# Message stage of a graph network: two rings in place of one, the difference of odd pairs completed in PSUM, DVE left with the even pairs

## The chip, the cores and the metric

The kernel runs on one core of a Trainium2 chip. The metric is the device time of one launch in microseconds (us), lower is better. The engines named here are PE (TensorE, matmuls into PSUM), DVE (VectorE), ACT (ScalarE), POOL (GpSimd) and SP (SyncE, which issues plain DMAs). PSUM is the memory that PE writes; it is read by DVE and ACT.

## The reference, cut to what matters

Two graph layers follow each other on 6250 nodes with 256 features and 100000 edges. The second one is the message layer, and the stage that is changed computes this for every edge (row, col):

```
xy   = clip(mink_dot(x[row], x[col]) + K, None, -EPS) - K
u    = x[col] + xy * x[row] * C
dist = sqrt(sqdist(x[row], x[col]))
x_local_tangent = proj_tan(dist * u / max(mink_norm(u), MIN_NORM), x[row])
h    = silu(concat(x_tangent[row], x_tangent[col], distances) @ att_w1 + att_b1)
att  = sigmoid(h @ att_w2 + att_b2) * edge_mask
agg  = segment_sum(x_local_tangent * att, row, N) / NORM_FACTOR
```

For an edge the kernel needs the node row of the far end (gathered by index), the node row of the near end (edges are sorted by it), their difference, a sum of squares of it, the attention input, and a weighted sum per near node.

## The kernel before

The message stage (`messages`) goes over the sorted edges in steps of 128 edges. Two steps (SPAN = 2) that share a block of near nodes are a **pair**; four pairs (SG = 4, eight steps, G = 8) are a **turn**, and two turns (WG = 2) a **window**. There are 110 turns, so 55 windows and 440 pairs. Every engine has its own program, written as a function `period(t)` for each turn t; engines meet by semaphores, and each works through its own program strictly in that order. Pairs are numbered p = 0 to 3 within a turn; 0 and 2 are called even, 1 and 3 odd.

- POOL gathers, for each step, 128 rows of 514 numbers from `d_xr` into a ring `far` of five turns (RING = 5), by `gather_pair`, L2216 to L2226. A row holds 257 numbers for the difference, one node term, and 256 for attention. A slot of the ring is freed by `out_in`, which PE sets at the very end of the pair's life.
- SP loads the index columns (`col`) and a row of local node numbers per edge (`hotT`); DVE turns `hotT` into a one-hot matrix (`hot_columns`, L2421).
- PE, `near(t, p)` (L2284 to L2306), spreads the near nodes' rows to the edges by one-hot matmuls: `near_a` (257 wide, L2301) and `near_c` (256 wide, L2302). For odd pairs an identity matmul (L2304) adds the gathered attention part onto `near_c` in PSUM. `near_a` has four banks, so two pairs fit; `near(t, p)` waits until what `near` wrote two pairs earlier has been read. An even pair takes four matmuls, an odd pair six. `sums(t, p)` (L2308 to L2322) adds up the finished edges per node, two matmuls (L2321).
- DVE, `differences` (L2403 to L2414): for every pair, gathered row plus `near_a`, in place in the ring (L2410), and for even pairs gathered part plus `near_c` (L2413). Further attention sums (L2443), weights (`hot_rows`, L2433), accumulation (`add`, L2454), and once per window the small chain `angles`, `radii`, `shares`.
- ACT: `silu` for every pair (L2346 from PSUM for odd, L2349 for even pairs), `squares` (L2361), and once per window `chain` (L2364 to L2374) between `silu(t, 1)` and `squares(t, 1)`: five short activations on 16 numbers per partition with three table loads.
- POOL, once per window: `place_a` (two copies), then `finish`, eleven small operations, each waiting for the one before.

In PE's program of a turn t these stand in a row: sums, near(t, 2), sums, near(t, 3), sums, near(t+1, 0), sums, near(t+1, 1). The sums are those of the turn LAG = 3 turns back.

Of the kernel before, what the change touches and what calls it, by code (L numbers as in the profile page):

```python
# [7 lines left out]
F32 = mybir.dt.float32  # L8
# [2103 lines left out]
def messages(nc, m, edges):  # L2112
# [8 lines left out]
    with Stage(nc, "ms") as ctx:  # L2121
# [3 lines left out]
        SLOT = G * XW  # L2125
        IN_AREA = 3
        more = sb("more", [P, (RING - IN_AREA) * SLOT])
        spare = [m.area[:, n * SLOT:(n + 1) * SLOT] for n in range(IN_AREA)] + [more[:, n * SLOT:(n + 1) * SLOT] for n in range(RING - IN_AREA)]
        far = [t.rearrange("p (k c) -> p k c", c=XW) for t in spare]
        rest = [IN_AREA * SLOT]  # L2130

        def rest_of_area(n):
# [3 lines left out]

        WSLOTS = BODY // WG
        r_aw2 = rest_of_area(DIM)
        given = rest_of_area(2 * WSLOTS * WSTEPS).rearrange("p (v w k) -> p v w k", v=2, w=WSLOTS)
# [3 lines left out]
        SQ, AL = (given[:, v] for v in range(2))  # L2143
# [14 lines left out]
        got = [ctx.gather_sem(m, f"got{h}") for h in range(RING)]  # L2158
        (c_in, made, hotT_in, near_in, apart, squared, v_in, silu_in, al_in, dv, ab_in, root_in, nn_in, norm_in, ex_in, z_in, ln_in,
         rden_in, a_in, pl, c_ready, weighted, out_in, summed) = (sem(n) for n in (  # L2160
             "c_in", "made", "hotT_in", "near_in", "apart", "squared", "v_in", "silu_in", "al_in", "dve", "ab_in", "root_in", "nn_in",
# [10 lines left out]
        def pair_before(t, p, back):  # L2172


            q, r = divmod(p - back, SG)
            return t.plus(q), r

        with nc.Block() as block:
            @block.sync
            def _(sp):  # L2180
# [15 lines left out]
                def fetch(t):  # L2196
                    fetch_col(t.plus(2))
# [6 lines left out]
                fetch_col(Turn(0, 0))  # L2204
                fetch_col(Turn(0, 1))
# [3 lines left out]
            def _(pool):  # L2209
# [7 lines left out]
                def gather_pair(t, p):  # L2217
                    if not t.exists():
                        return
                    if p == 0:  # L2220
                        reach(col_in[t.h], (t.i + 1) * 16)
                    if t.plus(-RING).exists():
                        reach(out_in, t.plus(-RING).n * SG + p + 1)
                    for k in (SPAN * p, SPAN * p + 1):
                        pool.indirect_dma_start(out=far[t.slot][:, k, :], out_offset=None, in_=m.d_xr,  # L2225
                                                in_offset=bass.IndirectOffsetOnAxis(ap=col[:, t.h, k, 0:1], axis=0)).then_inc(got[t.slot], 16)  # L2226

                def place_a(w):

                    reach(nn_in, w.window + 1)  # L2230
                    for t in (w, w.plus(1)):
                        k0 = (t.h % WG) * G
                        GP.tensor_copy(far[t.slot][:, :, DIM], A[:, k0:k0 + G]).then_inc(a_in, 1)

                def finish(w):

                    n = w.window
                    sm = PoolSmall(m, pool, GP, Links(pool, pl, n * PER))
                    reach(root_in, 2 * n + 2)
                    sm.ts(FLAG, A, 0.01, None, ALU.is_lt)  # L2240
                    sm.ts(S, A, 3.0 / 160, -1.0 / 12, ALU.mult, ALU.add)
                    sm.tt(S, S, A, ALU.mult)
                    sm.ts(S, S, 1.0, None, ALU.add)
                    sm.tt(S, S, ROOT, ALU.mult)
                    reach(ln_in, n + 1)
                    sm.tt(S, S, LN, ALU.subtract)
                    sm.tt(S, S, FLAG, ALU.mult)
                    sm.tt(S, S, LN, ALU.add)
                    sm.ts(S, S, math.sqrt(FAR), None, ALU.min)
                    reach(rden_in, 2 * n + 2)  # L2250
                    sm.tt(S, S, DEN, ALU.mult)
                    assert sm.ln.n == PER, sm.ln.n
# [5 lines left out]
                def period(t):  # L2258
# [3 lines left out]
                    if w:  # L2262
                        place_a(w)
                    gather_pair(t.plus(2), 1)
                    if w:
                        finish(w)
# [345 lines left out]
```

## Time and profile before

| | us |
|---|---|
| median of 3 runs | 4565.07 |
| lowest, highest | 4560.52, 4568.45 |
| the profiled execution | 4568.81 |
| its span in the trace | 4566.7 |
| message stage, first to last near matmul | 2562.0 to 4285 |

The message stage is a bit over a third of the span; the sorting and the attention stage are ahead of it, a short final stage follows. A fp32 matmul of the program stands in the trace as two records ("x2"). The duration of a PE record has the drain of the array in it, so records overlap; the pace is read from start to start. The granted clock of PE is given as a fraction: 1.00 is 2.4 GHz and 0.50 is 1.2 GHz.

### The profile page before, as it was taken

How to read it: one execution, taken by the hardware profiler on the slowest of the kernel's cores; microseconds unless marked ns; L12 is line 12 of the kernel's file. 1: busy time of each engine (PE TensorE's matmuls, PEld its weight loads, DVE VectorE, ACT ScalarE, POOL GpSimd, SP SyncE). 2: the span in 40 equal slices, each digit the busy share in tenths (PEclk: the TensorE clock that was granted, in tenths of full speed). 3: DMA queues.
4: the chain of work that ended last, by engine and by line, in shares of the span. 5: the costliest groups of instructions: out<-in, count | busy, mean ns of one | idle time of the engine just before them, and what ended most of it. 6: DMA issues, size and time to landing. Idle time of an engine off the chain costs nothing. (4 is left out here: it accounts for less than half of the span.)

```text
span 4566.7 us, 61946 instructions
## 1 busy us (share of the span) xinstructions
PE 3026.1 (66%) x12512; PEld 2401.1 (53%) x12513; DVE 3592.1 (79%) x9543; ACT 2065.8 (45%) x5079; POOL 2032.7 (45%) x2519
## 2 busy tenths in 40 slices
PE   1101111465887877778746688888888888888685
PEld 0101110454665655556635577676766767677554
DVE  6879998554999999999976477777777777777766
ACT  0013332002555555555546455555555555555356
POOL 1000000003777777777710466565656665565301
PEclk9997555787899999999978899999999999999888
DMA  0010000325887888887844566656556565665531
GB/s 7 0 37 0 0 0 16 91 80 160 243 240 243 241 238 240 240 243 238 247 112 132 167 172 173 167 160 172 164 169 171 164 170 161 173 173 161 127 81 45
DMA packets 294449, 664.33 MB, mean 145 GB/s; under 512 B 77025, under 2 KB 146335, under 8 KB 293869
## 3 DMA queue, kind: packets, MB, share of 16 engines
q0 software_dynamic: 141312, 463.96, 35.3%
q1 hardware_dynamic: 152813, 197.34, 15.4%
q14 instruction: 278, 2.28, 0.2%
q8 instruction: 46, 0.75, 0.1%
HBM read 616.23 MB, written 44.91 MB: 145 GB/s over the span
## 5 line engine op out<-in xcount | busy, mean ns | idle before, releaser
L1812 POOL DMA_INDIRECT big<-d_qv,at_col x880 | 930.5, 1057 | 572.7 <-DMA at_col<-by_dst_edge_cols 290.5
L2225 POOL DMA_INDIRECT big<-d_xr,ms_col x528 | 530.3, 1004 | 588.7 <-DMA ms_col<-by_src_edge_cols 259.2
L2301 PE MATMUL ms_near_a<-big,ms_hotT 128*128 x1760 | 575.0, 410 | 232.4 <-DMA big<-d_xr,ms_col 123.1
L2302 PE MATMUL ms_near_c<-big,ms_hotT 128*128 x1760 | 561.3, 402 | 0.0
L1858 PE MATMUL at_out<-at_pv,at_hot 128*128 128x264 f32 x1760 | 518.8, 421 | 4.9 <-DVE big L2024 3.1
L2301 PEld LDWEIGHTS ms_near_a<-big,ms_hotT 128*128 128x128 f32 x1760 | 345.6, 202 | 323.6 <-issue 276.1
L1838 PE MATMUL at_kx<-big 128*128 x1760 | 493.3, 407 | 31.8 <-ACT big L1912 23.2
L2225 POOL DMA_INDIRECT ms_more<-d_xr,ms_col x352 | 353.8, 1005 | 214.7 <-PE ms_out L2321 111.6
L1838 PEld LDWEIGHTS at_kx<-big 128*128 128x128 f32 x1760 | 350.8, 204 | 111.1 <-issue 54.2
L2302 PEld LDWEIGHTS ms_near_c<-big,ms_hotT 128*128 128x128 f32 x1760 | 357.6, 203 | 58.0
L2433 DVE TENSOR_SCALAR ms_hot<-ramp,ms_col,big 128x128 f32<-128x128 f32 x880 | 269.1, 374 | 145.1 <-POOL big L2255 143.4
L1858 PEld LDWEIGHTS at_out<-at_pv,at_hot 128*128 128x128 f32 x1760 | 335.1, 203 | 69.7 <-issue 10.5
L2003 DVE TENSOR_TENSOR big<-big,at_kx 128x512 f32<-128x512 f32 x440 | 297.2, 676 | 73.4 <-DMA big<-d_qv,at_col 41.5
L2321 PE MATMUL ms_out<-big,ms_hot 128*128 128x257 f32 x1056 | 280.6, 389 | 31.4 <-DVE ms_hot L2433 29.5
L2410 DVE TENSOR_TENSOR big<-big,ms_near_a 128x514 f32<-128x514 f32 x264 | 178.4, 676 | 117.5 <-DMA big<-d_xr,ms_col 94.3
L1922 ACT ACTIVATE at_hot<-ramp,at_col 128x128 f32<-128x128 f32 x880 | 267.4, 386 | 3.8 <-PE at_out L1858 3.8
L1982 DVE TENSOR_TENSOR at_pv<-big,at_pw 128x1024 f32<-128x1024 f32 x220 | 268.0, 1218 | 0.0
L2014 DVE TENSOR_REDUCE at_sc<-big 128x32 f32<-128x1024 f32 x220 | 265.4, 1207 | 0.1
L2361 ACT ACTIVATE ms_junk<-big 128x255 bf16<-128x255 f32 x528 | 211.7, 402 | 109.8 <-DVE big L2410 109.1
L2321 PEld LDWEIGHTS ms_out<-big,ms_hot 128*128 128x128 f32 x1056 | 201.7, 194 | 77.2 <-DVE ms_hot L2433 16.5
L532 POOL DMA_INDIRECT by_src_got<-by_src_rec,by_src_tile_i x4 | 3.8, 945 | 524.2 <-DVEq L402 523.3
L2024 DVE SCALAR_TENSOR_TENSOR big<-big,at_keep,at_out 128x264 f32 x440 | 211.6, 481 | 20.1 <-PE at_out L1858 10.2
(368 smaller groups left out, 6693.6 us busy)
## 6 DMA issues: line engine op xcount, KB each, us to landing
big<-by_dst_marks SPq DMA_DIRECT2D x110, 512.0 KB, 5.4
ms_hotT<-by_src_marks SPq DMA_DIRECT2D x110, 448.0 KB
big<-d_qv,at_col POOLq DMA_INDIRECT x880
d_qv<-big SPq DMA_DIRECT2D x5, 2240.0 KB, 9.1
big<-d_xr,ms_col POOLq DMA_INDIRECT x528, 4.2
ms_hotT<-by_src_marks SPq DMA_DIRECT2D x110, 60.0 KB
d_xr<-mid_hm SPq DMA_DIRECT2D x5, 1128.8 KB, 6.9
ms_more<-d_xr,ms_col POOLq DMA_INDIRECT x352, 4.2
```

The lines of the kernel that those rows point to most:

```text
L1812: pool.indirect_dma_start(out=ring[t.slot][:, k, :], out_offset=None, in_=m.d_qv, in_offset=bass.IndirectOffsetOnAxis(ap=col[:, t.h, k, 0: ...
L1838: last = TE.matmul(kx[:, p, k * DIM:(k + 1) * DIM], hotT[:, t.h % 2, (SPAN * p + k) * P:(SPAN * p + k + 1) * P], m.keys[:, bass.ds(at, DIM ...
L1858: last = TE.matmul(out[:, p % 2, 0:AW], hot[:, t.h % 2, j, :], pv[:, t.h % 2, j].rearrange("p h d -> p (h d)"), start=(k == 0), stop=(k == ...
L1922: A.activation(hot[:, t.h % 2, k, :], m.ramp[:, :], ACT.Abs, scale=-1.0, bias=col[:, t.h, k, 1:2].bitcast(F32)).then_inc(far_rows, 1)
L1982: V.tensor_tensor(pv[:, t.h % 2, k, :, 0:DH], ring[t.slot][:, k, DIM:2 * DIM].rearrange("p k (h d) -> p k h d", d=DH), pw[:, t.wslot, k0:k ...
L2003: V.tensor_tensor(prod[:, SPAN * p:SPAN * p + SPAN, :], ring[t.slot][:, SPAN * p:SPAN * p + SPAN, 0:DIM], kx[:, p, :].rearrange("p (a d) - ...
L2014: V.tensor_reduce(sc[:, k0:k0 + G // 2, :].rearrange("p k h -> p (k h)"), prod[:, k, :].rearrange("p k (h d) -> p (k h) d", d=DH), axis=AX ...
L2225: pool.indirect_dma_start(out=far[t.slot][:, k, :], out_offset=None, in_=m.d_xr, in_offset=bass.IndirectOffsetOnAxis(ap=col[:, t.h, k, 0:1 ...
L2301: TE.matmul(near_a[:, (SPAN * p + k) % 4, 0:TW], rows, m.tab_a[:, bass.ds(at, TW)], start=True, stop=True)
L2302: last = TE.matmul(near_c[:, p % 2, k * DIM:(k + 1) * DIM], rows, m.tab_c[:, bass.ds(at, DIM)], start=True, stop=p % 2 == 0)
L2321: last = TE.matmul(out[:, p % 2, 0:TW], hot[:, j, :], far[t.slot][:, j, 0:TW], start=(k == 0), stop=(k == SPAN - 1))
L2433: V.tensor_scalar(hot[:, k, :], m.ramp[:, :], col[:, t.h, k, 1:2].bitcast(F32), cs[:, t.wslot, at:at + 1], ALU.is_equal, ALU.mult).then_in ...
```

## The change

The one ring of five turns is split in two. The gathered rows go into a ring of ten pairs (`far_rows`), and each slot is freed when the pair's attention sums are done (`al_in`). The differences go into a second ring of five turns with rows of 257 (`dd`). Since the node term does not get a place in `dd`, ACT copies it out of the gathered row (`keep_node_term`) once per pair, and `place_a` becomes two copies in ACT's `chain`. For odd pairs PE adds the gathered 257 numbers onto `near_a` by the identity, and ACT copies the whole difference from PSUM into `dd`; DVE does `differences` for even pairs only. POOL's window chain is laced with six gathers, and its order is different. Gathers are issued by two more pairs ahead, waits for gathered rows are per pair, and `sums` and `hot_rows` run LATE = 4 turns back where they ran 3.

```diff
+        PAIRS, DSLOT, LATE = 10, G * TW, WG + 2
+                    if k == 0:
+                        before, q = pair_before(t, p, PAIRS)
+                        if before.exists():
+                            reach(al_in, before.n * G + SPAN * q + SPAN)
...
                     before, q = pair_before(t, p, 2)
                     if before.exists():
-                        pe.wait_ge(apart, before.n * SG + q + 1)
+                        pe.wait_ge(apart_odd if p % 2 else apart, before.n * (SG // 2) + q // 2 + 1)
...
                         if p % 2:
-                            last = TE.matmul(near_c[...], m.ident[:, :], far[t.slot][:, SPAN * p + k, XB:XW],
+                            TE.matmul(near_a[...], m.ident[:, :], far_rows(t, p)[:, k, 0:TW], start=False, stop=True)
+                            last = TE.matmul(near_c[...], m.ident[:, :], far_rows(t, p)[:, k, XB:XW],
                                              start=False, stop=True)
...
                 def squares(t, p):
-                    act.wait_ge(apart, t.n * SG + p + 1)
+                    if p % 2:
+                        AC.activation(dd[t.slot][:, SPAN * p:SPAN * p + SPAN, :], near_a[:, SPAN:2 * SPAN, 0:TW], ACT.Identity).then_inc(apart_odd, 1)
+                        act.wait_ge(apart_odd, t.n * (SG // 2) + p // 2 + 1)
+                    else:
+                        act.wait_ge(apart, t.n * (SG // 2) + p // 2 + 1)
...
                 def chain(w):
                     AC.activation(NN, NN, ACT.Sqrt).then_inc(norm_in, 1)
+                    for t in (w, w.plus(1)):
+                        AC.copy(dd[t.slot][:, :, DIM], A[:, (t.h % WG) * G:(t.h % WG) * G + G]).then_inc(a_in, 1)
...
                     for p in range(SG):
-                        differences(t, p)
+                        if p % 2 == 0:
+                            differences(t, p)
```

**PE, one odd pair between two `sums`.** Names: `hotT` is the one-hot matrix, `ident` the identity, `near_a` and `near_c` the two PSUM targets, `ms_out` the target of `sums`. The even pairs are unchanged. After the change:

```order
L2354 MATMUL ms_out<-big,ms_hot 128x257 x2
L2333 ISA
L2333 MATMUL ms_near_a<-big,ms_hotT 128x257
L2334 ISA
L2334 MATMUL ms_near_c<-big,ms_hotT 128x256
L2336 MATMUL ms_near_a<-big,ident 128x257
L2337 MATMUL ms_near_c<-big,ident 128x256
L2333 MATMUL ms_near_a<-big,ms_hotT 128x257
L2334 MATMUL ms_near_c<-big,ms_hotT 128x256
L2336 MATMUL ms_near_a<-big,ident 128x257
L2337 MATMUL ms_near_c<-big,ident 128x256
L2354 MATMUL ms_out<-big,ms_hot 128x257 x2
```

The two rows of L2336 are new, the others stood there before.

**ACT, from `silu(t, 1)` through the window's chain to `squares(t, 1)`, before:**

```order
L2346 ACTIVATE big<-ms_near_c 128x2x256
L2366 ISA
L2367 ACT_TABLE_LOAD
L2367 ACTIVATE big<-big 128x16
L2368 ACTIVATE big<-big 128x16
L2370 ACTIVATE big<-big 128x16
L2371 ISA
L2372 ACT_TABLE_LOAD
L2372 ACTIVATE big<-big,ms_nb 128x16
L2374 ACT_TABLE_LOAD
L2374 ACTIVATE big<-big,ones 128x16
```

The same place after the change, from the chain's first activation on:

```order
L2411 ACTIVATE big<-big 128x16
L2412 ACTIVATE big<-big 128x16
L2414 ACTIVATE big<-big 128x16
L2416 COPY ms_more<-big 128x8 x2
L2418 ACT_TABLE_LOAD
L2418 ACTIVATE big<-big,ms_nb 128x16
L2420 ACT_TABLE_LOAD
L2420 ACTIVATE big<-big,ones 128x16
L2396 ACTIVATE ms_more<-ms_near_a 128x514
L2405 ACTIVATE ms_junk,big<-ms_more 128x255 x2
L2376 COPY big<-big 128x2
```

The copies of L2416 came from POOL; the copy of L2396, which empties an odd pair's `near_a`, stands behind the chain, and the node term's copy of L2376 ahead of each silu.

**POOL, the window's chain after the change**, with the gathers (DMA rows of L2240) between its operations:

```order
L2259 TENSOR_SCALAR big<-big 128x16
L2260 TENSOR_SCALAR big<-big 128x16
L2240 DMA big<-d_xr,ms_col 128x514
L2263 TENSOR_TENSOR big<-big 128x16
L2240 DMA big<-d_xr,ms_col 128x514
L2266 TENSOR_SCALAR big<-big 128x16
L2240 DMA big<-d_xr,ms_col 128x514
L2269 TENSOR_TENSOR big<-big 128x16
L2240 DMA big<-d_xr,ms_col 128x514
```

Before, the eleven operations of the chain stood in a row with no gather between them.

## Rows read from the trace of the kernel before

**Rows 1.** The page, part 1: busy us (share of the span) xinstructions.

```profile
PE 3026.1 (66%) x12512; PEld 2401.1 (53%) x12513; DVE 3592.1 (79%) x9543; ACT 2065.8 (45%) x5079; POOL 2032.7 (45%) x2519
```

**Rows 2.** Busy time by stretch (x records), PEclk is the granted clock; 50 windows.

```profile
2708.20:4259.05 1550.85, 1321.73 (x5488) 1094.62 (x5488) 1188.90 (x4313) 855.64 (x2401) 941.38 (x1422) 0.93 0.60 168
```

**Rows 3.** Waits of PE in that stretch: us in total, times, longest.

```profile
PE ms_near_a L2301 <- DMA big<-d_xr,ms_col: 110.1, 30, 4.4
PE ms_near_a L2301 <- DMA ms_more<-d_xr,ms_col: 66.6, 19, 4.5
PE ms_out L2321 <- DVE ms_hot L2433: 35.4, 54, 3.1
```

**Rows 4.** Timeline of PE: start, us, line, records, [idle before <-releaser].

```profile
3309.42 1.03 PE L2321 MATMUL ms_out<-ms_more,ms_hot 128*128 128x257 f32 x4
3313.66 1.17 PE L2301 MATMUL ms_near_a<-big,ms_hotT 128*128 x2 [3.21 <-DMA ms_more<-d_xr,ms_col]
...
3317.61 0.60 PE L2304 MATMUL ms_near_c<-ms_more,ident 128*128 128x256 f32 x2
3318.04 1.03 PE L2321 MATMUL ms_out<-ms_more,ms_hot 128*128 128x257 f32 x4
3318.91 0.59 PE L2301 MATMUL ms_near_a<-big,ms_hotT 128*128 x2
...
3320.64 1.03 PE L2321 MATMUL ms_out<-big,ms_hot 128*128 128x257 f32 x4
3321.51 0.60 PE L2301 MATMUL ms_near_a<-big,ms_hotT 128*128 x2
```

**Rows 5.** Timeline of ACT at the same window, silu(t, 1), chain, squares(t, 1).

```profile
3318.24 0.60 ACT L2346 ACTIVATE ms_more<-ms_near_c 128x512 f32<-128x512 f32 x1 [1.93 <-PE ms_near_c L2304]
3318.86 1.28 ACT L2367 ACT_TABLE_LOAD   x1
...
3320.39 0.20 ACT L2370 ACTIVATE big<-big 128x16 f32<-128x16 f32 x1
3320.60 1.28 ACT L2372 ACT_TABLE_LOAD   x1
...
3323.52 0.31 ACT L2374 ACTIVATE big<-big,ones 128x16 f32<-128x16 f32 x1
3323.73 0.40 ACT L2361 ACTIVATE ms_junk<-ms_more 128x255 bf16<-128x255 f32 x1
```

**Rows 6.** PSUM reads by ACT: a copy in the final stage (ns min/median/max), L2346 by mean.

```profile
L1517 ACT ACTIVATE fin_sl<-fin_p x25: 594/603/604, 4351.0 to 4524.3; 128x512 f32<-128x512 f32 x25
L2346 ACT ACTIVATE big<-ms_near_c 128x512 f32<-128x512 f32 x132 | 77.4, 586 | 61.9 <-PE ms_near_c L2304 60.7
```

**Rows 7.** Stretches as in Rows 2, and PE's timeline ahead of two of them.

```profile
3314.00:3316.00 2.00, 2.00 (x6) 1.56 (x6) 1.97 (x11) 1.11 (x4) 1.70 (x2) 0.50 0.85 261
3990.00:3993.00 3.00, 3.00 (x9) 2.36 (x8) 3.00 (x12) 2.01 (x7) 2.50 (x4) 0.50 0.32 90
3671.00:3674.00 3.00, 3.00 (x16) 2.63 (x15) 3.00 (x12) 1.93 (x4) 1.16 (x2) 1.00 0.17 64
...
3988.18 1.13 PE L2321 MATMUL ms_out<-big,ms_hot 128*128 128x257 f32 x4 [2.52 <-DVE ms_hot L2433]
3670.60 1.13 PE L2321 MATMUL ms_out<-big,ms_hot 128*128 128x257 f32 x4 [2.01 <-DVE ms_hot L2433]
```

**Rows 8.** DVE: groups of instructions (busy us, mean ns, idle before), one wait.

```profile
L2410 DVE TENSOR_TENSOR big<-big,ms_near_a 128x514 f32<-128x514 f32 x264 | 178.4, 676 | 117.5 <-DMA big<-d_xr,ms_col 94.3
DVE ms_hot L2433 <- POOL big L2255: 134.6, 49, 3.9
```

**Rows 9.** POOL: its longest wait, and two rows of its timeline.

```profile
POOL big L2225 <- PE ms_out L2321: 166.6, 78, 6.0
3308.79 0.95 POOL L2225 DMA_INDIRECT ms_more<-d_xr,ms_col  x1 [0.30 <-issue]
3333.76 1.05 POOL L2225 DMA_INDIRECT big<-d_xr,ms_col  x1 [0.59 <-issue]
```

More of the change, by code:

```diff
@@ L2124, in messages @@
         sem = ctx.sem
[L2125 to L2130, printed above, removed]
+        PAIRS, DSLOT, LATE = 10, G * TW, WG + 2
+        far = m.area[:, 0:PAIRS * SPAN * XW].rearrange("p (k c) -> p k c", c=XW)
+        rest = [PAIRS * SPAN * XW]
+        more = sb("more", [P, (RING - 1) * DSLOT])
         def rest_of_area(n):
@@ L2215, in reach, with gather @@
                     pool.sem_inc(m.nothing, 1)
-                def gather_pair(t, p):
+                def gather(t, p, k):
                     if not t.exists():
                         return
[L2220 to L2235, printed above, removed]
-                    n = w.window
-                    sm = PoolSmall(m, pool, GP, Links(pool, pl, n * PER))
-                    reach(root_in, 2 * n + 2)
[L2240 to L2244, printed above, removed]
+                    if k == 0:
+                        if p == 0:
+                            reach(col_in[t.h], (t.i + 1) * 16)
+                        before, q = pair_before(t, p, PAIRS)
+                        if before.exists():
+                            reach(al_in, before.n * G + SPAN * q + SPAN)
@@ new lines, in gather, with gather_pair, finish_and_gather, settle @@
+                    pool.indirect_dma_start(out=far_rows(t, p)[:, k, :], out_offset=None, in_=m.d_xr,
+                                            in_offset=bass.IndirectOffsetOnAxis(ap=col[:, t.h, SPAN * p + k, 0:1], axis=0)).then_inc(got[far_slot(t, p)], 16)
+                def gather_pair(t, p):
+                    gather(t, p, 0)
+                    gather(t, p, 1)
+                def finish_and_gather(w, t):
+                    n = w.window
+                    two, three = t.plus(2), t.plus(3)
+                    ln = Links(pool, pl, n * PER)
+                    def settle():
+                        ln.wait()
+                        pool.sem_inc(m.nothing, 1)
+                    reach(root_in, 2 * n + 2)
+                    reach(nn_in, n + 1)
+                    ln.mark(GP.tensor_scalar(FLAG, A, 0.01, None, ALU.is_lt))
+                    ln.mark(GP.tensor_scalar(S, A, 3.0 / 160, -1.0 / 12, ALU.mult, ALU.add))
+                    gather(two, 2, 0)
+                    settle()
+                    ln.mark(GP.tensor_tensor(S, S, A, ALU.mult))
+                    gather(two, 2, 1)
+                    settle()
+                    ln.mark(GP.tensor_scalar(S, S, 1.0, None, ALU.add))
+                    gather(two, 3, 0)
+                    settle()
+                    ln.mark(GP.tensor_tensor(S, S, ROOT, ALU.mult))
+                    gather(two, 3, 1)
+                    settle()
@@ L2270, in _ @@
+                for n in range(2 * SG + 1):
                     gather_pair(Turn(0, n // SG), n % SG)
@@ L2320, in sums @@
                         j = SPAN * p + k
-                        last = TE.matmul(out[:, p % 2, 0:TW], hot[:, j, :], far[t.slot][:, j, 0:TW], start=(k == 0), stop=(k == SPAN - 1))
+                        last = TE.matmul(out[:, p % 2, 0:TW], hot[:, j, :], dd[t.slot][:, j, 0:TW], start=(k == 0), stop=(k == SPAN - 1))
                     last.then_inc(out_in, 1)
                 def period(t):
-                    old = t.plus(-LAG)
+                    old = t.plus(-LATE)
                     for p in range(SG):
@@ L2360, in squares @@
                         at = (t.h % WG) * G + SPAN * p + k
-                        AC.activation(junk[:, k, 1:DIM], far[t.slot][:, SPAN * p + k, 1:DIM], ACT.Square,
+                        AC.activation(junk[:, k, 1:DIM], dd[t.slot][:, SPAN * p + k, 1:DIM], ACT.Square,
                                       accum_out=SQ[:, t.wslot, at:at + 1]).then_inc(squared, 1)
```

101 lines of the change are left out of this document (59 added, 42 removed).

## The prediction

> **What bounds the kernel now.** I read the busy shares first, and they mislead: DVE has the most work over the whole span and PE comes second [rows 1], but that is a mean over stages. So I went to the stage that is changed, and there to a regular stretch of 50 windows. It lasts 1550.85 us, 31.0 us per window; in it PE is busy 1321.7 us, DVE 1188.9, POOL 941.4 and ACT 855.6 [rows 2]. PE is the bound, at 85%. What the reader should look for next is what fills the other 15%. Of PE's waits [rows 3] the gathered rows make up 110.1 + 66.6 = 176.7 us in 49 waits, one per window and 3.6 us each; the wait of `sums` for DVE's weights makes 35.4 us. With about 0.3 us of small ones that is 4.6 us per window.
>
> The work itself: from start to start, the four records of `sums` take 3318.91 - 3318.04 = 0.87 us and the eight of an even pair 1.73 us [rows 4], which is 0.2165 us per record or 0.433 us per matmul. A window has four even pairs (4 matmuls), four odd ones (6) and eight sums (2), 56 matmuls, so 24.2 us. Then 31.0 = 24.2 + 4.6 + 2.2. The rest of 2.2 us is the drain ahead of each wait (about 0.17 us, three waits) and the clock. After the wait of 3.21 us PE ran at 0.50, the level of 1.2 GHz [rows 7], and the odd pair that takes 6 x 0.433 = 2.6 us took 3318.04 - 3313.66 = 4.38 us [rows 4]: 1.8 us lost per window.
>
> **What the change takes away.** (1) The gathered rows come too late now because POOL waits for `sums` to free a slot, 166.6 us into one of its two buffers alone [rows 9]. After the change a slot is freed by the attention sums, and ten pairs make 10/8 of a window, about 40 us, while a pair needs two gathers (start to start 0.95 + 0.30 = 1.25 us each [rows 9]), a few us to land and some 8 us until its attention sums. I put this wait at nothing, -3.6 us per window. (2) The weights are needed one turn later (15 us), and they were late by 134.6/49 = 2.7 us on DVE [rows 8]. That wait goes too, about -0.8 us per window on PE with the small ones. (3) DVE loses four operations of 0.68 us per window [rows 8], which on an engine at 77% of the stage is worth nothing by itself.
>
> **What it adds on PE.** Two identity matmuls of 257 columns per odd pair, eight per window: 8 x 0.433 = 3.5 us. Nothing hides them, since they stand in PE's own row. PE's floor is then 64 x 0.433 = 27.7 us per window. With (1) and (2) and nothing else it would be 27.9, a gain of 3.1 us per window. The decision lies in the next term.
>
> **The wait it adds.** `near(t, 3)` must find the banks of odd pair (t, 1) empty. Until now DVE emptied them and ACT's `silu(t, 1)` the other half, both ahead of the chain. Now the copy that empties `near_a` stands on ACT behind the chain, so once per window PE waits for the chain. Behind the waiting `near(t, 3)` are all of PE's later sums and pairs, and behind these DVE and ACT.
> Take as zero the drained end of `near(t, 1)`, here 3317.61 + 0.60 = 3318.21 [rows 4]. ACT starts silu at 3318.24 [rows 5], +0.03. The new node term copy ahead of it is a short activation; the nearest is one of 16 numbers, 0.20 us by itself, 0.11 when the next overlaps it [rows 5]: I take 0.15. Silu until the first table load 0.62, from there until the chain is done 3323.73 - 3318.86 = 4.87. The two copies that came from POOL: 0.11 to 0.20 each, 0.3 together. The new copy of 128x514 out of PSUM: 0.59 to 0.60 by the two nearest rows [rows 6], and 0.05 to hand over. Sum 6.6 us. PE meanwhile has one sums, one even pair and one sums, which end 3.3 us after the zero (3321.51 - 3318.21 [rows 4]). So `near(t, 3)` starts 3.3 us late. Bounds: copies free and 0.55 us for the large one give 2.9, all of them at twice my value and DVE late for the chain by 0.5 give 4.7.
> Can something else hold ACT less? The chain cannot start earlier, it stands behind `silu(t, 1)`, which waits for the end of `near(t, 1)`. DVE's part comes in time: after the end of `near(t, 0)` it has 1.2 us of differences, 0.7 of attention sums and some 2.5 of `angles`, done 4.4 us later, while ACT ends `silu(t, 1)` 4.3 + 0.8 = 5.1 us after it (PE needs 3.46 + 0.87 for the odd pair and the sums ahead of it). At (t+1, 1) and (t, 3) no chain is in between and the copy comes within 1.5 us, under 3.3 us of PE work: no wait there.
>
> The Trainium skill speaks on this term ("ScalarE: Activation LUTs", section "What ACT_TABLE_LOAD costs"): a switch of tables costs a load of 1283 ns and a drain of about 1380 ns, 2.66 us in all. The load agrees with the row (1.28 us); the drain does not show here, since the load starts 0.02 us after the 0.60 us activation ended and the next load 0.01 us after 0.20 us. By the page's price the chain would take some 4 us more and the wait would be 7 us; I go by the rows.
>
> **The clock.** The added wait shows as about 3.2 us of idle PE. Of PE's waits in this stage of 2.5 us and more, the shortest of them 2.52 us, all but one were followed by a stretch at 0.50, and the shorter ones were not; one of each kind stands at 3988 and 3670, with the stretch behind it [rows 7]. The odd pair at 3313.66 lost 1.8 us. I take 1.7 for a wait that is a little shorter than most of those before; bounds 0 and 2.2.
>
> **The sum.** Per window 27.7 + 3.3 + 1.7 + 0.1 for small waits = 32.8 us, against 31.0: +1.8, or for 55 windows +97 us (with 1.7 it is +93; I take +95). At the start of the stage PE waits for one pair's rows in place of a turn's: four gathers fewer, 4 x 1.25 = -5 us. At the end one more turn of sums is left over, at 0.9 to 1.3 us a pair partly beside the last chain: +2 us. Sum +92. The profiled execution took 4568.8, so it would take 4661; the median is 3.7 us lower, which gives **4657 us**, 2% slower.
>
> ACT's own load is no bound: 855.6/50 = 17.1 us plus four copies of 0.6 and ten short ones of 0.15 makes 21 of 32.8. DMA moves the same bytes in more time.
>
> **The rivals.**
> (a) The wait is there, the clock stays up. Then the window is 31.1 us, +0.1 x 55 - 3 = +3 us: **4568**, no change. It needs a wait under 2.5 us, or 3 us that count as too short. For it: the phase at which PE stops. Against: every wait of 2.5 to 3.2 us save for one was followed by a fall. Chance 0.08.
> (b) PE runs back to back. The window is 27.9 us, 3.1 x 55 = 170 us less, with the start 173: **4392**. It decides at 3.3 us: only if ACT is through from `near(t, 1)` to the large copy within that time, while the chain alone takes 4.87. Partly so, by a shorter chain or an earlier start that I overlook, anything from 4400 to 4550. Chance 0.12 for the two.
> (c) POOL becomes the bound. Its window chain now alternates six gathers with operations: a gather after a small operation comes 0.59 in place of 0.30 us after it [rows 9], so a step is about 0.95 + 0.25 + 0.22 + 0.59 = 2.0 us, six make 12; ten gathers more 12.5, the last operations 2.5: 27 us of 32.8, and each pair waits for the attention sums. If a step costs 3 us (a wait in it, or the operation drained first), POOL needs 33 us and its waits come on top: 34 us per window, +3 x 55 = +165, **4730**. Against: the ring's slack of some 20 us. Chance 0.16, with all else that makes it slower still, as the load of `hotT` coming late for `hot_columns`, which now has 6 to 9 us where it had 12.
> (d) That the change does not do what it says: excluded by the order of the instructions, where L2336 and L2396 stand.
>
> **How the numbers follow.** The forecast has 0.64, with 4620 to 4700 by its bounds (window 32.1 to 33.6). About 9 us (0.2%) is what a measurement of this kernel can tell from no change. Slower by more: 0.64 + 0.16 = 0.80. Same: 0.08. Faster: 0.12. The range must hold 0.8: 0.62 of the forecast, (a) whole, and the larger part of (c), so 4560 to 4735.
>
> **What would show it.** PE's waits: none for gathered rows, one per window of about 3.2 us of `near_a` for ACT's copy of L2396, and its mean at 0.60 us. PE records in the stage go from 112 to 128 per window. The granted clock stays near 0.93, with one fall per window. DVE's wait for POOL is gone, and DVE waits for PE and ACT. If the wait per window is under 2.5 us, or no fall follows, I am wrong towards (a); if PE's longest wait is another one, towards (c).

## The result, and the profile after

The changed kernel took 4676.47 us (median of 4 runs, 4661.82 to 4688.16), the kernel before 4563.21 us (4 runs, 4560.52 to 4568.45). The ratio is 1.0245, with a 95% interval of 1.0213 to 1.0278: 2.4% slower. The forecast was 4657 us in a range of 4560 to 4735. The profiled execution took 4671.57 us (span 4669.7), 103 us more than that of before, where the sum had +92.

The busy times of the page, part 1 (us, share of the span, instructions), to be read against [rows 1]:

```profile
PE 3200.0 (69%) x13392; PEld 2577.2 (55%) x13393; DVE 3488.8 (75%) x9323; ACT 2249.2 (48%) x5849; POOL 2045.1 (44%) x2409
```

DVE has 220 instructions and 103 us less; PE has 880 more records of matmuls and ACT 770 more instructions: 440 short copies, 220 large ones and the 110 that POOL had. These are the groups of part 5 that were added (records, busy us, mean ns, idle time before):

```profile
L2336 PE MATMUL ms_near_a<-big,ident 128*128 128x257 f32 x880 | 291.2, 415 | 0.0
L2376 ACT COPY big<-big 128x2 f32<-128x2 f32 x440 | 84.3, 192 | 675.3 <-PE ms_near_c L2337 341.2
```

The regular stretch, here 53 windows (us, then busy time and records of PE, weight load, DVE, ACT and POOL, granted clock, DMA share, GB/s), answers [rows 2]:

```profile
2623.48:4363.20 1739.72, 1565.93 (x6657) 1331.33 (x6656) 1166.30 (x4372) 1080.89 (x3277) 1005.34 (x1407) 0.93 0.58 159
```

That is 1739.72/53 = 32.8 us per window, where [rows 2] had 31.0. PE is busy 90% of it. What fills the rest is in PE's waits over the whole stage (2560 to 4400; us in total, times, longest):

```profile
PE ms_near_a L2333 <- ACT ms_more L2396: 144.2, 44, 4.8
PE ms_near_a L2333 <- ACT big L2396: 24.1, 10, 3.3
PE ms_near_a L2333 <- DVE ms_hotT L2463: 17.6, 1, 17.6
PE ms_out L2354 <- DVE ms_hot L2475: 17.5, 11, 3.4
PE ms_near_a L2333 <- DMA big<-d_xr,ms_col: 2.5, 2, 1.7
```

[rows 3] has the regular stretch of before; over the whole stage (2560 to 4300) the same waits there were:

```profile
PE ms_near_a L2301 <- DMA big<-d_xr,ms_col: 123.1, 33, 6.6
PE ms_near_a L2301 <- DMA ms_more<-d_xr,ms_col: 73.4, 21, 4.5
PE ms_out L2321 <- DVE ms_hot L2433: 39.3, 57, 3.1
```

The waits for gathered rows, 123.1 + 73.4 = 196.5 us before, are gone but for 2.5 us at the start. In their place PE waits for ACT's large copy, 144.2 + 24.1 = 168.3 us in 54 waits, one per window: 3.1 us each. The weights hold PE for 17.5 us in place of 39.3.

One such wait can be followed through both engines. PE's timeline (start, us, line, tile, records, idle time before and its releaser), from the end of the odd pair (t, 1):

```profile
3123.24 0.60 PE L2337 MATMUL ms_near_c<-big,ident 128*128 128x256 f32 x2
3123.68 1.03 PE L2354 MATMUL ms_out<-ms_more,ms_hot 128*128 128x257 f32 x4
3124.55 0.59 PE L2333 MATMUL ms_near_a<-big,ms_hotT 128*128 x2
...
3126.28 1.03 PE L2354 MATMUL ms_out<-big,ms_hot 128*128 128x257 f32 x4
3130.57 0.70 PE L2333 MATMUL ms_near_a<-big,ms_hotT 128*128 x2 [3.27 <-ACT ms_more L2396]
```

ACT's timeline in the same time:

```profile
3123.88 0.19 ACT L2376 COPY big<-big 128x2 f32<-128x2 f32 x1 [1.49 <-PE ms_near_c L2337]
3123.98 0.59 ACT L2385 ACTIVATE big<-ms_near_c 128x512 f32<-128x512 f32 x1
3124.59 1.28 ACT L2411 ACT_TABLE_LOAD   x1
...
3126.22 0.29 ACT L2416 COPY ms_more<-big 128x8 f32<-128x8 f32 x2
3126.52 1.28 ACT L2418 ACT_TABLE_LOAD   x1
...
3129.44 0.31 ACT L2420 ACTIVATE big<-big,ones 128x16 f32<-128x16 f32 x1
3129.65 0.58 ACT L2396 ACTIVATE ms_more<-ms_near_a 128x514 f32<-128x514 f32 x1
```

`near(t, 1)` ends at 3123.24 + 0.60 = 3123.84, and PE has work until 3126.28 + 1.03 = 3127.31. ACT starts 0.04 us after the pair's end, goes through silu and the chain with no gap, and starts the copy at 3129.65; PE starts 0.92 us after that. PE then goes on within 0.34 us of the copy's end at 3130.23: ACT is what it waits for.

### The profile page after: what moved, and what is told of

It reads as the page before. It is cut to its first block and busy times, and to the rows that moved or that the text cites. A ratio compares the mean times of both kernels' runs of the same rounds, so it can differ in the third digit from the quotient of the medians.

```text
span 4669.7 us, 63970 instructions
## 1 busy us (share of the span) xinstructions
PE 3200.0 (69%) x13392; PEld 2577.2 (55%) x13393; DVE 3488.8 (75%) x9323; ACT 2249.2 (48%) x5849; POOL 2045.1 (44%) x2409
## 5 line engine op out<-in xcount | busy, mean ns | idle before, releaser
L2240 POOL DMA_INDIRECT big<-d_xr,ms_col x880 | 902.6, 1026 | 868.7 <-DVE big L2485 406.2
L2333 PE MATMUL ms_near_a<-big,ms_hotT 128*128 x1760 | 568.9, 406 | 188.5 <-ACT ms_more L2396 144.2
L2496 DVE SCALAR_TENSOR_TENSOR big<-big,ms_keep,ms_out 128x257 f32 x440 | 210.5, 478 | 290.8 <-PE ms_out L2354 278.6
L2485 DVE CUSTOM_DVE_ANT_0 big<-big 128x256 f32<-128x256 f32 x880 | 337.6, 421 | 101.5 <-ACT big L2389 101.0
L2376 ACT COPY big<-big 128x2 f32<-128x2 f32 x440 | 84.3, 192 | 675.3 <-PE ms_near_c L2337 341.2
L2354 PE MATMUL ms_out<-ms_more,ms_hot 128*128 128x257 f32 x1408 | 366.8, 384 | 20.1 <-DVE ms_hot L2475 20.0
L2354 PEld LDWEIGHTS ms_out<-ms_more,ms_hot 128*128 128x128 f32 x1408 | 267.5, 191 | 65.5 <-DVE big L2496 16.5
L2405 ACT ACTIVATE ms_junk<-ms_more 128x255 bf16<-128x255 f32 x704 | 283.5, 403 | 16.8
L2336 PE MATMUL ms_near_a<-big,ident 128*128 128x257 f32 x880 | 291.2, 415 | 0.0
L2337 PE MATMUL ms_near_c<-big,ident 128*128 128x256 f32 x880 | 282.4, 404 | 0.0
```

The costliest lines, as they stand in the source:

```text
L2240: pool.indirect_dma_start(out=far_rows(t, p)[:, k, :], out_offset=None, in_=m.d_xr, in_offset=bass.IndirectOffsetOnAxis(ap=col[:, t.h, SPA ...
L2333: TE.matmul(near_a[:, (SPAN * p + k) % 4, 0:TW], rows, m.tab_a[:, bass.ds(at, TW)], start=True, stop=p % 2 == 0)
L2336: TE.matmul(near_a[:, (SPAN * p + k) % 4, 0:TW], m.ident[:, :], far_rows(t, p)[:, k, 0:TW], start=False, stop=True)
L2337: last = TE.matmul(near_c[:, p % 2, k * DIM:(k + 1) * DIM], m.ident[:, :], far_rows(t, p)[:, k, XB:XW], start=False, stop=True)
L2354: last = TE.matmul(out[:, p % 2, 0:TW], hot[:, j, :], dd[t.slot][:, j, 0:TW], start=(k == 0), stop=(k == SPAN - 1))
L2405: AC.activation(junk[:, k, 1:DIM], dd[t.slot][:, SPAN * p + k, 1:DIM], ACT.Square, accum_out=SQ[:, t.wslot, at:at + 1]).then_inc(squared, 1)
```

## Experiments

The theory: PE loses the time because the copy that empties the odd banks stands behind ACT's chain, 3.3 us per window, and because the clock falls after that idle time, some 1.6 us more; the identity matmuls cost their own 3.5 us. The rivals: the identity matmuls alone make it slower; the wait is a sign of something else (gathers, POOL, a full DVE) that would come up in its place; the clock has nothing to do with it.

The runs came in three groups. The kernel before took 4573 us in the first; in the second and third it took 4897 and 4946 us. Most of the excess lies in a stage that the change does not touch, and its cause is not known (last section), so ratios to the kernel before of the same group are compared there, and no absolute times across groups.

### The copy ahead of the chain

```diff
                         AC.activation(rows, near_c[:, p % 2, :]..., ACT.Silu).then_inc(silu_in, 1)
+                        AC.activation(dd[t.slot][...], near_a[:, SPAN:2 * SPAN, 0:TW], ACT.Identity).then_inc(apart_odd, 1)
...
                     if p % 2:
-                        AC.activation(dd[t.slot][...], near_a[:, SPAN:2 * SPAN, 0:TW], ACT.Identity).then_inc(apart_odd, 1)
                         act.wait_ge(apart_odd, t.n * (SG // 2) + p // 2 + 1)
```

> The changed kernel with one move: ACT's copy that empties an odd pair's near_a stands right behind that pair's silu, so at p = 1 ahead of the window's chain. My theory (PE waits 3.3 us per window because this copy stands behind the chain, and the clock falls after the wait for a further 1.6 us): both terms go, and a smaller wait comes up at near(t+1, 1), since ACT is behind after its chain; by the walk with measured durations 1.2 us per window. Window 27.9 + 1.2 = 29.1 us against 32.8, so 4676 - 3.7 x 55 = about 4475 us (4430 to 4530), PE's longest wait under 2 us and hardly any time at 0.50 of the clock. Rival 'PE's added matmuls alone make it slower': the move changes nothing, 4676. Rival 'POOL with its laced chain is next': window of 31 us or more, 4580, and PE or DVE waits for gathered rows or for POOL.

Measured: 4449.90 us, ratio 0.9723 (0.9698 to 0.9747), 5% less than the changed kernel from one instruction moved. The stretch 2700 to 4100:

```profile
2700.00:4100.00 1400.00, 1345.85 (x6144) 1158.92 (x6143) 1067.00 (x4031) 982.41 (x3023) 923.11 (x1296) 1.00 0.68 183
```

PE's waits in it:

```profile
PE ms_near_a L2333 <- ACT ms_more L2386: 38.2, 38, 1.0
PE ms_out L2354 <- DVE ms_hot L2475: 13.2, 8, 3.2
```

The wait behind the chain is gone. A new one of 1.0 us per window comes at the next turn's odd pair, for the copy of (t, 3), and the clock does not fall after it (1.00 over the stretch). The waits at 3105.14 and 3134.14 lie 29.0 us apart: 27.7 + 1.0 + 0.2 for the drain, and some 0.1 for the first matmul after the wait. PE does all its matmuls, the identity ones too, and is 96% busy. So the place of the copy, not the matmuls, decided the sign, and neither POOL nor DVE was a hidden bound at 29 us.

### PE kept at work through the wait

```diff
                     before, q = pair_before(t, p, 2)
+                    if p == 3 and window_of(t) and before.exists():
+                        pe.wait_ge(silu_in, before.n * SG + q + 1)
+                        for _ in range(7):
+                            TE.matmul(near_c[:, 1, 0:DIM], m.ident[:, :], m.tab_c[:, 0:DIM], start=True, stop=True)
```

> The changed kernel with seven idle matmuls of 256 columns by the identity (7 x 0.433 = 3.0 us) ahead of near(t, 3) in the turns with a chain, into the PSUM bank that silu(t, 1) has just freed; their result is overwritten. They lie inside PE's wait and leave the wait for ACT's copy as it is, only the idle time goes from 3.3 to 0.2 to 0.3 us. Theory (part of the loss is the clock that falls after the wait): the clock stays at 1.00, windows take 31.2 us as those in the changed kernel after which it did not fall, so 4676 - 1.6 x 55 = about 4590 us (4570 to 4610). Rival 'the clock costs nothing, the wait is all': 4676 or, if the idle matmuls delay near(t, 3), a bit more.

Measured: 4570.86 us, ratio 0.9993 (0.9980 to 1.0006), 0.025 of the time or 115 us less than the changed kernel, with 3.0 us more of matmuls in the same wait. The same stretch:

```profile
2700.00:4100.00 1400.00, 1385.06 (x6322) 1191.92 (x6321) 998.70 (x3733) 921.89 (x2803) 870.93 (x1202) 1.00 0.63 170
```

The expectation gave the clock 1.6 x 55 = 88 of these 115 us. The first and the last `near` record stand at 2566.2 and 4281.9 here, 2561.9 and 4383.9 after the change: 1715.7 for 1822.0 us, 1.9 us less per window. The changed kernel itself shows the clock's share. These are three windows in a row, from the end of one wait for ACT to the end of the next (3.26 or 3.27 us each):

```profile
3099.32:3130.57 31.25, 27.98 (x128) 24.12 (x129) 20.90 (x79) 20.80 (x64) 19.66 (x27) 1.00 0.62 168
3130.57:3163.52 32.95, 29.68 (x129) 25.30 (x129) 24.24 (x94) 20.82 (x64) 19.23 (x29) 0.93 0.59 163
3163.52:3197.61 34.09, 30.82 (x128) 26.17 (x129) 20.70 (x77) 20.79 (x64) 18.71 (x27) 0.90 0.57 155
```

The work and the wait are the same; the windows differ by the clock alone, by 0, 1.70 and 2.84 us. Their mean over the stretch, 32.8 - 31.25, is 1.6 us. With the filled wait two windows last 31.06 us each (the fillers start at 3101.63, 3132.69 and 3163.75), 0.19 us less than the window of 31.25. ACT's copy still decides when `near(t, 3)` starts: in the second of them it ends at 3135.20 + 0.58 = 3135.78 and PE goes on at 3135.93, after 0.15 us where it took 0.34 from idleness. So of the 1.9 us per window 1.6 are the clock and 0.2 this quicker start; the 0.1 that is left was not located. That the clock costs this much is shown: the wait for the copy was kept, and only its idleness taken away.

### Two rings without the part in PSUM

DVE does all pairs again, as before; the rings stay.

```diff
-                        TE.matmul(near_a[:, ..., 0:TW], rows, m.tab_a[...], start=True, stop=p % 2 == 0)
+                        TE.matmul(near_a[:, ..., 0:TW], rows, m.tab_a[...], start=True, stop=True)
                         if p % 2:
-                            TE.matmul(near_a[:, ..., 0:TW], m.ident[:, :], far_rows(t, p)[:, k, 0:TW], start=False, stop=True)
...
-                        AC.activation(dd[t.slot][...], near_a[:, SPAN:2 * SPAN, 0:TW], ACT.Identity).then_inc(apart_odd, 1)
...
-                        if p % 2 == 0:
-                            differences(t, p)
+                        differences(t, p)
```

> The changed kernel without its PSUM part: two rings, gathers laced into POOL's chain, later sums, all as in the change, but DVE makes the difference of odd pairs too, out of the ring of gathered rows and near_a into the ring of differences; no identity matmul on near_a, no large copy on ACT. Theory (the ring part removes the waits of the kernel before, the PSUM part brings PE's 3.5 us and the wait for the chain): PE's work is 24.2 us, DVE's about 24.7, POOL's about 27; the largest is POOL or the handover between PE and DVE, window 26 to 28.5 us, so 4563 - 4 x 55 = about 4345 us (4280 to 4430), faster than both. Rival 'the rings themselves cost as much as they give' (POOL bound at over 31 us, or DVE, which now has no slack): 4560 or more.

Measured: 4453.95 us, ratio 0.9735 (0.9715 to 0.9755). The direction is right and the size is missed by 109 us. PE's largest wait from 2700 to 4100:

```profile
PE ms_out L2353 <- DVE ms_hot L2476: 123.3, 123, 2.2
```

The busy times of that stretch:

```profile
2700.00:4100.00 1400.00, 1229.44 (x5298) 988.58 (x5296) 1155.30 (x4168) 867.16 (x2794) 902.51 (x1278) 0.99 0.67 180
```

DVE's group of `hot_columns` in it (busy us, mean ns, idle before and its releaser):

```profile
L2464 DVE TENSOR_SCALAR ms_hotT<-ms_hotT,lane 127x1024 f32<-127x1024 f32 x95 | 73.5, 774 | 189.5 <-DMA ms_hotT<-by_src_weights 189.4
```

One instance in DVE's timeline:

```profile
3054.52 0.75 DVE L2464 TENSOR_SCALAR ms_hotT<-ms_hotT,lane 127x1024 f32<-127x1024 f32 x1 [3.24 <-DMA ms_hotT<-by_src_weights]
```

With 24.2 us of matmuls in a 29-us window, PE now loses to DVE: `hot_columns` stands in DVE's row after pair 1 and waits 2.0 us in each of 95 turns for the load of `hotT`, which by the program is issued only when PE has left that buffer. The weights of `sums` stand behind it. Rival (c) had named this wait, for a window of 33 us; in the changed kernel DVE has less of it (68.6 us in the whole stage) and PE does not feel it.

From the first to the last `near` record the stage takes 1597.4 us here and 1596.5 us with the copy ahead of the chain, against 1722.8 before the change. So the gain over the kernel before is there without the part in PSUM, and that part, with its copy in the better place, neither adds to it nor takes from it. What in the rest gives the gain (the two rings, the gathers laced into POOL's chain, the later sums) was not taken apart.

### The identity matmuls left out

The far part is missing from the differences of odd pairs; everything else stays.

```diff
-                            TE.matmul(near_a[:, ..., 0:TW], m.ident[:, :], far_rows(t, p)[:, k, 0:TW], start=False, stop=True)
```

> The changed kernel without the identity matmul that adds the gathered 257 numbers onto near_a for odd pairs; the copy out of PSUM stays, so odd pairs' differences lack their far part. This takes 3.5 us of PE work per window and nothing else. Theory (PE's own work is on the path all through the window, save the stretch between near(t, 1) and near(t, 3), where no odd pair lies): all 3.5 us come off, wait for ACT unchanged at 3.3 us once per window: 4676 - 3.5 x 55 = about 4485 us (4460 to 4510). Rival 'PE's added work is hidden in the wait': under 60 us come off, the wait grows.

Measured: 4498.75 us, ratio 0.9828 (0.9799 to 0.9857): 0.0417 less than 1.0245, or 190 us give or take 20, against 8 x 0.433 x 55 = 190 us by the sum. The traces say somewhat less: from the first to the last `near` record 1652.4 us (2563.0 to 4215.4) for 1822.0, 170 us or 3.1 us per window. The wait for ACT stays (stretch 2700 to 4100):

```profile
PE ms_near_a L2333 <- ACT ms_more L2395: 125.3, 36, 5.5
PE ms_near_a L2333 <- ACT big L2395: 23.9, 10, 3.1
```

149.2 us in 46 waits is 3.2 us each: the wait does not grow when the matmuls go, so nothing of them was hidden in it, and they cost nine tenths of their time or all of it. What makes the 0.4 us per window between the traces and the sum was not separated. With the copy ahead of the chain the matmuls stand in PE's work of 27.7 us too; there the waits that the rings took away were worth more than they cost.

### A chain that is longer by 1.06 us

Two activations of 512 columns that nobody reads stand at the end of the chain.

```diff
                     AC.activation(LN, Z, ACT.Ln, bias=one).then_inc(ln_in, 1)
+                    for j in range(2):
+                        AC.activation(blank[:, j, :], m.tab_c[:, 0:2 * DIM], ACT.Square).then_inc(extra, 1)
```

> The changed kernel with two extra activations of 512 numbers on ACT at the end of the window's chain, ahead of the copy that empties near_a (about 0.53 us each, start to start, 1.06 together; their results are not used). Nothing else. Theory (the path is near(t, 1), silu, chain, copy, near(t, 3)): each us on this path is a us per window, PE's wait grows from 3.27 to 4.3 us and the whole from 1.0245 of the kernel before by 1.06 x 55 = 58 us, 0.013, give or take 0.005 for where the clock falls: 1.037. Rival (ACT has 11 us per window to spare, so the copy's place is harmless and the loss is PE's added work): no change, 1.0245.

Measured, in the second group: ratio 1.0342 (1.0275 to 1.0408). PE's waits for ACT in two regular windows:

```profile
3647.17 1.07 PE L2335 MATMUL ms_near_a<-big,ms_hotT 128*128 x2 [4.30 <-ACT ms_more L2398]
3681.15 0.92 PE L2335 MATMUL ms_near_a<-big,ms_hotT 128*128 x2 [4.30 <-ACT ms_more L2398]
```

4.30 us where it was 3.27: a chain longer by 1.06 us (expected; 3646.26 - 3645.22 = 1.04 us in ACT's row there) makes PE wait 1.03 us more. What is added to the chain reaches PE nearly one to one, so the chain lies on the path and has no slack. The ratio alone would not show it: it rises by 0.0097, or 44 us, where 0.013 was expected, and its interval touches that of the changed kernel.

### Can the rings give more?

Three edits on the two faster forms. The first loads and turns `hotT` in halves, so that each half can be refilled half a turn earlier:

```diff
-                    if t.plus(-2).exists():
-                        sp.wait_ge(near_in, t.plus(-2).n * SG + SG)
+                    for j in range(2):
+                        if t.plus(-2).exists():
+                            sp.wait_ge(near_in, t.plus(-2).n * SG + 2 * j + 2)
...
-                        if p == 1:
-                            hot_columns(t.plus(1))
+                        if p % 2:
+                            hot_columns(t.plus(1), p // 2)
```

On top of the rings alone, in the second and the third group:

> The rings alone (DVE makes all differences), and hotT loaded and turned into a one-hot matrix in two halves, so that each half has some six pairs of time in place of four. In the run of the rings alone DVE waited 189.4 us for hotT in 1400 us, 4.0 us per window of 29.3. Theory (this wait is what kept the rings at 29.3 us in place of 26 to 28.5): it goes, DVE needs about 25.4 us of its own, POOL about 27, the window is 27 us (25.5 to 28), 4454 - 2.3 x 55 = about 4327 us (4270 to 4390). Rival (DVE is full anyway and the wait only stands where its slack is): within 30 us of 4454.

> The rings alone with hotT in halves once more, now with the rings alone beside it. On the chip of the last job, where the attention stage, the same in all kernels, took 300 us longer than elsewhere, its message stage took 1606 us, no less than that of the rings alone elsewhere (1597). Theory (the wait for hotT kept the rings at 29.3 us): 30 us or more faster than the rings alone beside it, down to 27 us per window (-127 us). Rival (DVE or POOL is full and the wait for hotT stands in its slack, or the smaller DMAs and the split operation cost what they give): within 30 us of the rings alone beside it.

Measured: 0.9704 (0.9652 to 0.9756) and 0.9758 (0.9719 to 0.9797). The rings alone were run again beside the second of these:

> The rings alone once more, to stand beside the two with hotT in halves on the same chip: ratio 0.973 to the kernel before, as in the first job, if the chip is like that one.

Measured: 0.9836 (0.9792 to 0.9880). Halves give 43 us in that group (4818.30 for 4861.18 us), 31 us of it between the first and the last `near` record (1630.4 for 1661.9 us), and DVE's wait for `hotT` falls to a third (3200 to 4500). With halves:

```profile
DVE ms_hotT L2468 <- DMA ms_hotT<-by_src_weights: 35.9, 35, 2.1
```

Without:

```profile
DVE ms_hotT L2464 <- DMA ms_hotT<-by_src_weights: 108.9, 54, 3.6
```

That is far from the 127 us that the theory allowed and hardly more than the 30 of the rival: with two thirds of the wait for `hotT` gone the stage still takes 1630.4/55 = 29.6 us per window, not 27. With halves DVE waits 50.8 + 12.4 us for PE's pairs in the same stretch, which are not among its longer waits without.

The second edit goes half the way of the change on top of it: of a turn's two odd pairs, (t, 3) is completed in PSUM and copied by ACT, (t, 1) is done by DVE, so that the banks of (t, 1) never wait for the chain.

```diff
-                        if p % 2:
+                        if p == 3:
                             TE.matmul(near_a[:, ..., 0:TW], m.ident[:, :], far_rows(t, p)[:, k, 0:TW], start=False, stop=True)
...
-                        if p % 2 == 0:
+                        if p < 3:
                             differences(t, p)
```

> As the rings with hotT in halves, but of the two odd pairs of a turn the second one (p = 3) has its difference completed in PSUM by PE and copied by ACT, and the first one (p = 1), behind whose silu the chain stands, stays with DVE. PE has 24.2 + 1.7 = 25.9 us per window, DVE 25.4 - 2.4/2 = 24.2, and the wait for the chain isn't there. Theory (the PSUM part is harmless where no chain lies between the pair and its copy): window equal to that of the rings with hotT in halves if POOL's 27 us are the bound (about 4327), up to 1 us less (4275) if DVE was. Rival (the large copy on ACT holds PE wherever it stands): 60 us or more slower than the rings with hotT in halves, with waits of near_a for ACT.

> The mixed kernel once more (pair 3 completed in PSUM and copied by ACT, pair 1 by DVE, hotT in halves). Theory (the PSUM part is harmless where no chain lies between the pair and its copy): not more than 30 us slower than the rings with hotT in halves beside it. Rival (the large copy holds PE wherever it stands): 60 us or more slower, with waits of near_a for ACT. In the last job it was 51 us slower, with waits of 0.7 us per window for ACT; so a value between is likely.

Measured: 0.9802 (0.9746 to 0.9857) and 0.9835 (0.9797 to 0.9874), 50 us more than the rings with halves in both groups (4806.51 for 4755.33, 4867.81 for 4818.30). That lies between the theory (30 at most) and the rival (60 or more). PE still waits for the copy of (t, 3), 37.8 us in 17 waits from 3200 to 4500. Four identity matmuls are 1.73 us per window, 95 us for 55, so about half of their price does not show. Whether DVE's relief gave it back or PE had idle time for them was not separated.

The third sets halves on the copy ahead of the chain, and the last reorders ACT in the turns with a chain, so that `silu(t, 2)` and `silu(t, 3)` with its copy come ahead of two `squares`:

```diff
                     if w:
                         chain(w)
+                        silu(t, 2)
+                        silu(t, 3)
+                        squares(t, 1)
+                        squares(t, 2)
```

> The kernel with the copy ahead of the chain, and hotT in halves besides. There PE is the bound (27.7 us of work in a window of 29.0, and 1.0 us of waiting for ACT), so the earlier hotT is worth nothing: 4450 us give or take 10. If the wait for hotT is a bound there too, it gets 20 us or more faster.

> The kernel with the copy ahead of the chain, and in turns with a chain ACT does silu(t, 2), silu(t, 3) with its copy before the squares of pairs 1 and 2, which read only the ring in SBUF. In the run with the copy ahead of the chain PE still waited 1.0 us per window for the copy of pair 3, since ACT was behind after the chain. Theory (that wait is ACT's backlog of two groups of squares, 1.6 us): it goes, the window falls from 29.0 to 28.0 us, and the ratio to the kernel before from 0.972 to 0.972 - 55/4563 = 0.960. Rival (another wait takes its place: DVE's or POOL's): no change, 0.972.

Measured: 0.9817 (0.9757 to 0.9877) and 0.9795 (0.9757 to 0.9832), both short of what was expected (0.973 and 0.960). The first has no run of the copy ahead of the chain in its own group to stand beside, so nothing follows for the halves. In the second the wait it was to remove is still there, and DVE waits long for `hotT` (PE and DVE, 3200 to 4500):

```profile
PE ms_near_a L2333 <- ACT ms_more L2386: 44.1, 46, 1.6
DVE ms_hotT L2468 <- DMA ms_hotT<-by_src_weights: 159.9, 68, 4.1
```

46 waits of 1.0 us, though in one window ACT comes from the last step of the chain to that copy in 2.82 us where it took 4.41. In that window ACT began its part 2.1 us after `near(t, 1)` had ended, and no row says what it waited for. It is no single case: from 3200 to 4500 ACT has 54.0 + 30.0 us in 29 such waits ahead of L2376, where the copy ahead of the chain had none in the first group (2700 to 4100). So this run speaks neither for nor against the theory, and the reason of those waits stays open.

## Why the prediction was right

**The waits that vanish.** (1) 3.6 us per window for gathered rows: gone, as forecast; 2.5 us in all are left. (2) The late weights: DVE does not wait for POOL in this stage any more. PE still waits for weights, 17.5 us in place of 39.3 over the stage, mostly at every fifth window, where the loop's body ends, so some 0.3 us of the 0.8 stayed. (3) DVE's relief was put at nothing by itself, and nothing speaks against it: with the copy in the better place the stage takes as long as with the rings alone (1596.5 and 1597.4 us).

**PE's work.** 27.7 us per window by the sum. The undisturbed window of 31.25 us less the wait of 3.27 is 27.98 us, which is PE's busy time in it. Leaving the matmuls out gave 190 us by the ratios and 170 us by the traces, for 190 in the term. PE has 128 records per window, as forecast.

**The new wait.** Forecast 3.3 us, measured 3.27 in a regular window. The pieces were less exact than the sum, and their errors cancel:

| piece, us | forecast | measured |
|---|---|---|
| ACT starts after the pair's end | 0.03 | 0.04 |
| node term copy | 0.15 | 0.10 |
| silu to the first table load | 0.62 | 0.61 |
| chain with its two copies | 4.87 + 0.3 | 5.06 |
| large copy and handover to PE | 0.60 + 0.05 | 0.58 + 0.34 |
| whole path | 6.6 | 6.7 |
| PE's work meanwhile | 3.3 | 3.5 |

The handover was mis-sized, 0.05 for 0.34 us; 0.15 us of it is left when PE does not idle before it (the filled wait above). Of the 3.5 us of PE's work 0.17 are the drain, which the prediction books apart: counted as it counts, from the start that PE could have had (3126.28 + 0.87 = 3127.15), `near(t, 3)` comes 3.42 us late for 3.3. That the pieces cancel to 0.1 us is luck in part. The chain has no drain at its table loads here either: the load at 3124.59 starts 0.02 us after silu's end at 3124.57. The Trainium skill ("ScalarE: Activation LUTs", section "What ACT_TABLE_LOAD costs") states some 1.38 us of drain for each of them, by which, as an estimate from that figure, the wait would have been 7 us; the trace does not agree, and the rows decided rightly for 3.3.

**The clock.** Forecast 1.7 us per window, measured 1.6, and the granted clock is 0.93 before and after. The picture behind it was half right: not every wait is followed by a fall. Of the three windows above with equal waits one has none, one loses 1.70 and one 2.84 us; over the stretch some nine of the 53 have none. The mean was right because the dearer falls made up for the missing ones, and that is luck: the prediction had no reason for either. Rival (a), a clock that stays up, holds in single windows only. Its price was right too: the filled wait gave 0.9993, or 4562 us of 4565, close to the 4568 us of (a).

**The sum.** +1.8 us per window was forecast and measured (32.8 for 31.0). From the first to the last `near` record the stage takes 1822.0 us (2561.9 to 4383.9) for 1722.8 before (2562.0 to 4284.8), +99, against +95 - 5. Half of these 9 us is a slip in the prediction's sum: 1.8 x 55 is 99, not the 97 that it wrote or the 95 that it took. The other half is the start of the stage, which gained nothing. Beyond 55 regular windows the stage has 16.6 us now and had 16.9 before. PE's first wait for rows is 0.82 us where it was 6.56, as forecast, but 1.7 us more for rows came after it, and 4.8 us for the first chain, 1.5 more than a regular one. From the end of the last pair's matmuls to the end of the last `add` the stage needs 29.7 us in place of 23.4 (4385.54 to 4415.21, and 4286.06 to 4309.48), +6.3 where +2 stood: the leftover turn has nothing beside it. The end of the last pair came 9.5 us later than forecast; with 4.3 us here, and 2.7 us less outside the stage, that is the 11 by which 103 passes 92. The median then rose by 113 us, 10 more than the profiled execution, whose time is below the median after and above it before.

**The rivals.** (b) fell at its own test: ACT needs 6.7 us, not 3.3. But it was the nearest to what the rings can do: with the copy ahead of the chain the window is 29.0 us where (b) had 27.9. (c) did not occur: after the first windows PE never waits for POOL's gathers, and the wait for `hotT` reached PE once, at the start (17.6 us, 16.7 before the change). It has its place in the shorter window of the rings alone.

## What to carry over

An operation that empties a buffer belongs ahead of a long in-order sequence on its engine, not behind it: here one copy moved ahead of a 5-us chain was worth 5% of the whole kernel. Before moving work to an engine with spare time, follow the path from the last input to the released buffer through everything queued there, and set it against the work that the waiting engine has meanwhile. A new wait on TensorE has two prices, its length and the clock after it, and the second can be half of the first.

## What the runs showed of the hardware

- Equal waits of 3.27 us on PE cost 0, 1.70 or 2.84 us more in clock (31.25, 32.95 and 34.09 us for a window with the same work). Seven matmuls with no use in each wait kept the clock at 1.00 and took 115 us off the kernel (0.9993 for 1.0245).
- A wait of 1.0 us per window was followed by no fall: the granted clock of the whole stretch is 1.00 with the copy ahead of the chain. One wait of 3.19 us for the weights in that run (3154.32 to 3157.51) was followed by a fall: 0.57 from 3158 to 3162.
- ACT's short copies cost 0.10 us of its time where the next instruction overlaps them (3123.88 to 3123.98), though each is recorded with 0.19; from the end of a PSUM copy on ACT to the matmul that waited for it pass 0.34 us after an idle PE, and 0.15 us where other matmuls had run up to it (3135.78 to 3135.93).
- The gain from the rings differs between the groups: 0.9735 in the first, 0.9836 in the third. The same kernel (the rings alone) needs 1597 us there and 1662 us here for the message stage, and 1218 and 1564 us for the matmuls of the attention stage, which is the same in all kernels (`at_kx`, 1091.1 to 2309.1 and 1092.9 to 2657.2). In 1000 us of that stage PE did 3262 records in the profiled execution of the kernel before, and 2552 in the third group (rings with halves). The engines' busy time and the share of the DMA engines fell together with the bytes moved (0.80 for 240 GB/s, 0.63 for 188), so the rows show fewer transfers and not slower ones; what held the engines up is not shown:

```profile
1200.00:2200.00 1000.00, 795.71 (x3262) 598.32 (x3261) 941.28 (x1895) 552.31 (x1179) 766.25 (x721) 0.94 0.80 240
...
1200.00:2200.00 1000.00, 702.32 (x2552) 522.91 (x2552) 745.98 (x1491) 431.34 (x922) 569.45 (x562) 0.83 0.63 188
```
